# Mamba scan: partitions hold 4 states of 32 channels, sums over states in four column tiles, delta and delta u copied four times through DRAM

## The reference

```
xz = norm(x) @ in_proj_w.T ; x, z = xz[:512], xz[512:]         # 512 channels
u  = silu(conv4(x) + conv_b)
dt_lo, B, C = u @ x_proj_w.T                                    # 64, 16 and 16 wide
delta = softplus(dt_lo @ dt_proj_w.T + dt_proj_b)               # a value per channel and step
step t, for each of 512 channels d and 16 states n:
    h[d,n] = exp(delta[t,d] * A[d,n]) * h[d,n] + delta[t,d] * u[t,d] * B[t,n]
    y[t,d] = sum over n of h[d,n] * C[t,n]
out = ((y + u * D) * silu(z)) @ out_proj_w.T ; x1 = x + out
```

## Time and profile before

| | us |
|---|---|
| median of 3 runs | 3668.91 (3668.2 to 3672.8) |
| the profiled execution, its own time | 3673.93 |
| its span, first to last instruction | 3672.1 |
| busy in the span: PE, DVE, ACT, POOL | 3076.9, 2359.1, 1541.0, 2411.9 |

### The profile page before, as it was taken

The page is one execution under the profiler, slowest core; times in us unless marked ns, Lnnn a source line. Parts: engine busy times, 40 slices in busy tenths (PEclk is TensorE's granted clock), DMA queues, the critical chain, the costliest instruction groups (busy, mean ns, idle before and its releaser), DMA issues. The chain is left out here.

```text
span 3672.1 us, 40492 instructions
## 1 busy us (share of the span) xinstructions
PE 3076.9 (84%) x13154; PEld 1668.5 (45%) x13154; DVE 2359.1 (64%) x2473; ACT 1541.0 (42%) x2519; POOL 2411.9 (66%) x1493
## 2 busy tenths in 40 slices
PE   5988899889988998899887359996888888529998
PEld 2344344334434443444343236663656666416665
DVE  1898888888888888888889552211555555462221
ACT  3555554555555456545654112222334343202221
POOL 1898888888988888878989146662333343217663
PEclk8999999999989999999999669998999999859999
DMA  3022312220232032203221104442011111203343
GB/s 124 32 87 110 116 36 86 110 109 25 103 110 87 34 115 110 87 35 115 104 87 40 52 27 82 83 80 53 25 46 40 46 40 36 75 22 73 81 81 34
DMA packets 120038, 260.62 MB, mean 71 GB/s; under 512 B 15345, under 2 KB 91121, under 8 KB 103378
## 3 DMA queue, kind: packets, MB, share of 16 engines
q1 hardware_dynamic: 91218, 225.29, 16.9%
q0 software_dynamic: 28672, 33.64, 6.0%
HBM read 206.46 MB, written 52.43 MB: 71 GB/s over the span
## 5 line engine op out<-in xcount | busy, mean ns | idle before, releaser
L472 POOL TENSOR_TENSOR m_dbu<-m_du,m_bc 128x1024 f32<-128x1024 f32 x512 | 1192.7, 2357 | 10.3 <-DVE m_dah L552 10.1
L662 PE MATMUL m_y<-m_hc,m_ident 128*128 128x512 f32 x2048 | 992.6, 617 | 20.2 <-POOL m_hc L479 11.3
L552 DVE TENSOR_TENSOR_SCAN m_dah<-m_dah,m_dbu 128x1024 f32<-128x1024 f32 x352 | 804.9, 2287 | 153.9 <-ACT m_dah L297 145.4
L297 ACT ACTIVATE m_dah<-m_delta,m_a_neg 128x512 f32<-128x512 f32 x1024 | 661.9, 681 | 405.6 <-DVE m_hc L563 374.1
L662 PEld LDWEIGHTS m_y<-m_hc,m_ident 128*128 128x128 f32 x2048 | 404.7, 200 | 533.3 <-issue 495.8
L479 POOL TENSOR_TENSOR m_hc<-m_hc,m_bc 128x1024 f32<-128x1024 f32 x160 | 376.5, 2353 | 231.2 <-DVE m_hc L552 231.1
L563 DVE TENSOR_TENSOR m_hc<-m_dah,m_bc 128x1024 f32<-128x1024 f32 x352 | 429.1, 1219 | 14.6 <-PE m_y L662 3.5
L552 DVE TENSOR_TENSOR_SCAN m_hc<-m_dah,m_dbu 128x1024 f32<-128x1024 f32 x160 | 365.1, 2282 | 38.4 <-ACT m_dah L297 38.2
L662 PE MATMUL m_wk<-m_xnT,m_w_in 128*128 128x512 f32 x512 | 244.7, 601 | 11.5 <-DVE m_cw_diag L615 8.8
L662 PE MATMUL m_wk<-m_xs,m_cw_diag 128*128 128x512 f32 x512 | 244.9, 602 | 3.4 <-ACT m_xs L332 3.4
L1136 PE MATMUL f_h<-f_xgT,f_w 128*128 128x512 f32 x512 | 222.3, 595 | 0.0
(11 more groups left out here) (288 smaller groups left out, 4454.7 us busy)
## 6 DMA issues: line engine op xcount, KB each, us to landing
m_bc<-bcd SPq DMA_DIRECT2D x64, 2048.0 KB, 8.2
f_w<-in_w SPq DMA_DIRECT2D x24, 512.0 KB, 4.6
g_w<-in_w SPq DMA_DIRECT2D x24, 512.0 KB, 4.6
m_xt<-in_x SPq DMA_DIRECT2D x16, 512.0 KB, 8.2
m_xr<-in_x SPq DMA_DIRECT2D x16, 512.0 KB, 10.0
x<-m_xr SPq DMA_DIRECT2D x16, 512.0 KB, 3.0
xn<-m_yg SPq DMA_DIRECT2D x16, 512.0 KB, 9.3
t_xt<-x SPq DMA_DIRECT2D x16, 512.0 KB, 3.9
```

The costliest lines, as they stand in the source:

```text
L297: last = nc.scalar.activation(dah[:, un % 2, i * T:(i + 1) * T], delta[:, par, dt, :], ACT.Exp, scale=a_neg[:, dt, n:n + 1])
L472: nc.gpsimd.tensor_tensor(dbu[:, un % RING, :, :], du[:, 2 * hf:2 * hf + 2, :], bc[:, 0, n:n + 1, :].to_broadcast([P, 2, T]), ALU.mult).th ...
L552: nc.vector.tensor_tensor_scan(to, dah[:, un % 2, :], dbu[:, un % RING, :, :].rearrange("p i t -> p (i t)"), 0.0, ALU.mult, ALU.add).then_ ...
L662: return nc.tensor.matmul(out, lhsT, rhs, start=first, stop=last)
```

## The change

The partitions now hold 4 states of 32 channels each (partition = 32 * n + d). A *chunk* c is 128 channels, 8 units. A unit is four states (`st` of `NSET` = 4 sets) of two of the chunk's four blocks q of 32 channels. The work of a unit on ACT, POOL and DVE keeps its shape of 128 x 1024.

- The exponentials and first products need delta and du with each block of 32 channels repeated for the 4 states. `store_dd` stores a half of delta and du (two DMAs of 512 KB) to the DRAM tensor ddd, `load_rep` reads a chunk back four times into `delta_r` and `du_r` (8 DMAs, 2 MB in all), two chunks deep. delta itself has one buffer instead of two.
- B and C need one row for each set of 4 states on a partition: 0.5 MB a set instead of 2 MB a group, in four DMAs.
- The sum over the 4 states of a partition block is a product with `fold` (128 x 32, ones where partition % 32 is the column). Its 32 result rows are one of four column places of y. `total` is now one step for two units, with one product for each of the four blocks q. `d_term`, in slots 2, 10, 18 and 26, and `gate_scores` are written in the same 32-column pieces. y alternates by chunk, and the gate works on one chunk at a time (after scans 15, 19, 29 and 3 of the next batch).
- `ON_POOL` has 8 units instead of 10. Most unit numbers of the helpers are others; xn1t and sc have buffers of their own, so the gate no longer waits for stores.

```diff
+NM = UN // 2
+SB = 32
+NQ = P // SB
+NL = P // SB
+NSET = NS // NL
+NREP = NL
+ON_POOL = (1, 4, 7, 8, 17, 19, 23, 27)
...
-        delta = s.sb("delta", [P, 2, KD, T])
+        delta = s.sb("delta", [P, KD, T])
         du = s.sb("du", [P, KD, T])
 
-        bc = s.sb("bc", [P, 2, NS, T])
+
+        delta_r = s.sb("delta_r", [P, 2, NQ, T])
+        du_r = s.sb("du_r", [P, 2, NQ, T])
+        bc = s.sb("bc", [P, 2, NSET, T])
...
+        xn1t = s.sb("xn1t", [P, TJ, C])
...
-            def load_bc(b, g):
-                if g == 0:
+            def load_bc(b, st):
+                if st == 0:
                     wait_alone(sp_, S["st_bc"], b * 16 + 16, S["tick"])
                 if not below(b, 1):
-                    last = NS + 4 * g + 3
-                    wait_alone(sp_, S["dBu"], (b - 1) * UN + last + 1, S["tick"])
-                    wait_alone(sp_, S["hP"], (b - 1) * NP_ + P_BEFORE[last + 1], S["tick"])
-                    wait_alone(sp_, S["hD"], (b - 1) * ND_ + D_BEFORE[last + 1], S["tick"])
-                rows = slice(4 * g, 4 * g + 4)
-                src = bcd.rearrange("(k n) t -> k n t", k=2)[:, rows, :]
-                sp_.dma_start(bc[:, :, rows, :], src.partition_broadcast(P)).then_inc(S[f"ld_bc{g}"], 16)
+                    last = UN - 2 * (NSET - st) + 2
+                    wait_alone(sp_, S["dBu"], (b - 1) * UN + last, S["tick"])
+                    wait_alone(sp_, S["hP"], (b - 1) * NP_ + P_BEFORE[last], S["tick"])
+                    wait_alone(sp_, S["hD"], (b - 1) * ND_ + D_BEFORE[last], S["tick"])
+                src = bcd.rearrange("(k s n) t -> s n k t", k=2, n=NL)
+                for n in range(NL):
+                    sp_.dma_start(bc[n * SB:(n + 1) * SB, :, st, :], src[st, n].partition_broadcast(SB))\
+                        .then_inc(S[f"ld_bc{st}"], 16)
+
+            def store_dd(b, hf):
+                two = slice(2 * hf, 2 * hf + 2)
+                wait_alone(sp_, S["dz"], b * 2 + hf + 1, S["tick"])
+                if not below(b, 1):
+                    for c in (2 * hf, 2 * hf + 1):
+                        wait_alone(sp_, S[f"ld_r{c}"], b * 2 * 16 * NREP, S["tick"])
+                for k, tile in enumerate((delta, du)):
+                    sp_.dma_start(ddd[k, hf].rearrange("k p t -> p k t"), tile[:, two, :]).then_inc(S[f"st_dd{hf}"], 16)
+
+            def load_rep(b, c):
+
+
+                wait_alone(sp_, S[f"st_dd{c // 2}"], b * 32 + 32, S["tick"])
+                if c >= 2 or not below(b, 1):
+                    used = b * UN + 8 * (c - 1)
+                    wait_alone(sp_, S["dA"], used, S["tick"])
+                    wait_alone(sp_, S["dBu"], used, S["tick"])
+                for k, tile in enumerate((delta_r, du_r)):
+                    src = ddd[k, c // 2, c % 2].rearrange("(q d) t -> d q t", q=NQ)
+                    for n in range(NL):
+                        sp_.dma_start(tile[n * SB:(n + 1) * SB, c % 2, :, :], src).then_inc(S[f"ld_r{c}"], 16)
...
+                if post:
+                    load_rep(b, 1)
                 if ahead(b):
                     wait_alone(sp_, S["tr"], b * 2 + 4, S["tick"])
                     load_x(b + 2)
+                store_dd(b, 1)
+                load_rep(b, 2)
                 if post:
                     store_x1(b - 1)
-                if prep:
-                    store_bc(b + 1)
-                    load_bc(b + 1, 0)
+                load_rep(b, 3)
                 if post:
                     store_xn1(b - 1)
                     load_xr(b)
                 if prep:
+                    store_bc(b + 1)
+                    load_bc(b + 1, 0)
+                    store_dd(b + 1, 0)
+                    load_rep(b + 1, 0)
                     load_bc(b + 1, 1)
-                    load_bc(b + 1, 2)
                 if post:
                     store_sc(b - 1)
                 if prep:
+                    load_bc(b + 1, 2)
                     load_bc(b + 1, 3)
...
-            def scan_exp(b, par, un):
-                hf, n = un // NS, un % NS
-                if n == 0:
-                    act.wait_ge(S["dz"], b * 2 + hf + 1)
+            def scan_exp(b, un):
+                c, st, h = un // 8, un % 8 // 2, un % 2
+                if un % 8 == 0:
+                    act.wait_ge(S[f"ld_r{c}"], (b + 1) * 2 * 16 * NREP)
                 if un >= 2 or not below(b, 1):
                     v, vb = (un - 2) % UN, b - (un < 2)
                     if v in ON_POOL:
@@ -293,11 +329,10 @@
                     else:
                         act.wait_ge(S["hD"], vb * ND_ + D_BEFORE[v] + 1)
...
-                    if post and un in (16, 17):
-                        out_norm3(b - 1, (16, 17).index(un))
+                    if post and un in (20, 27):
+                        out_norm3(b - 1, (20, 27).index(un))
...
-            def times_b(b, par, un):
-                hf, n = un // NS, un % NS
-                if n == 0:
-                    pool.wait_ge(S["du"], b * 2 + hf + 1)
-                if hf == 0 and n % 4 == 0:
-                    pool.wait_ge(S[f"ld_bc{n // 4}"], b * 16 + 16)
+            def times_b(b, un):
+                c, st, h = un // 8, un % 8 // 2, un % 2
+                if un % 8 == 0:
+                    pool.wait_ge(S[f"ld_r{c}"], (b + 1) * 2 * 16 * NREP)
+                if c == 0 and h == 0:
+                    pool.wait_ge(S[f"ld_bc{st}"], (b + 1) * 16 * NL)
                 if not below(b * UN + un, RING):
                     pool.wait_ge(S["scan"], b * UN + un - RING + 1)
-                nc.gpsimd.tensor_tensor(dbu[:, un % RING, :, :], du[:, 2 * hf:2 * hf + 2, :],
-                                        bc[:, 0, n:n + 1, :].to_broadcast([P, 2, T]),
+                nc.gpsimd.tensor_tensor(dbu[:, un % RING, :, :], du_r[:, c % 2, 2 * h:2 * h + 2, :],
+                                        bc[:, 0, st:st + 1, :].to_broadcast([P, 2, T]),
...
                     if post:
-                        if un == 2:
+                        if un == 0:
                             mk_du(b, par, 1)
...
-                    if prep and un == 30:
+                    if prep and un == 28:
                         mk_du(b + 1, 1 - par, 0)
...
-            def gate(b, par, hf):
-                dve.wait_ge(S["sum"], b * UN + (hf + 1) * NS)
-                if hf == 0:
+            def gate(b, par, c):
+                dve.wait_ge(S["sum"], b * NM + c * NSET + NSET)
+                if c == 0:
                     dve.wait_ge(S["sz"], b + 1)
                 if not below(b, 1):
-                    if hf == 0:
+                    if c == 0:
                         dve.wait_ge(S["op"], b * 2)
-                    else:
-                        dve.wait_ge(S["pt"], b * 2)
-                        dve.wait_ge(S["st_xn1"], b * 16)
-                two = slice(2 * hf, 2 * hf + 2)
-                nc.vector.tensor_tensor(yg[:, two, :], y[:], sz[:, par, two, :], ALU.mult).then_inc(S["yg"], 1)
+                nc.vector.tensor_tensor(yg[:, c, :], y[:, c % 2, :], sz[:, par, c, :], ALU.mult).then_inc(S["yg"], 1)
...
+                    if un in (15, 19, 29):
+                        gate(b, par, (15, 19, 29).index(un))
                     if post:
-                        if un == 1:
-                            gate(b - 1, 1 - par, 1)
-                        if un in (9, 10):
-                            residual(b - 1, (9, 10).index(un))
-                        if un in (10, 11):
-                            out_norm1(b - 1, (10, 11).index(un))
-                        if un == 14:
+                        if un == 3:
+                            gate(b - 1, 1 - par, 3)
...
-            def d_term(b, par, hf):
-                if hf == 0:
-                    pe.wait_ge(S["u"], b + 1)
-                if not below(b * 2 + hf, 1):
-                    pe.wait_ge(S["yg"], b * 2 + hf)
-                for i in range(2):
-                    last = mm(y[:, i, :], d_diag[:, 2 * hf + i, :], u[:, par, 2 * hf + i, :], True, False)
-                last.then_inc(S["dm"], 1)
-
-            def total(b, un):
-                wait_h(pe, b, un)
-                for i in range(2):
-                    last = mm(y[:, i, :], ident[:], hc[:, un % RING, i, :], False, un % NS == NS - 1)
+            def d_term(b, par, c):
+                if c == 0:
+                    wait_alone(pe, S["u"], b + 1, S["tick"])
+                if not below(b * 4 + c, 2):
+                    wait_alone(pe, S["yg"], b * 4 + c - 1, S["tick"])
+                for q in range(NQ):
+                    nc.tensor.matmul(y[q * SB:(q + 1) * SB, c % 2, :], d_diag[:, c, q * SB:(q + 1) * SB], u[:, par, c, :],
+                                     start=True, stop=False, skip_group_check=True)
+
+            def total(b, m):
+                c, st = m // NSET, m % NSET
+                for un in (2 * m, 2 * m + 1):
+                    if un in ON_POOL:
```

(23 more changed lines are left out.)

189 lines of the change are left out of this document (97 added, 92 removed).

## The result

The changed kernel takes 3692.1 us (median of four runs, 3687.5 to 3693.2), the kernel before 3668.6 on the same chip: ratio 1.006 [1.0043, 1.0077]. It is 23.5 us slower, where 50 us faster was forecast.

The account below looks back on a forecast made before the run. PE was taken to lead in a ring of waits, with DVE beneath. -189 (DVE) + 43 (waits inside batches) + 90 (edge) + 5 (start) = -51; 3673.9 - 51 = 3623, less 5: 3618, called 3620; range 3545 to 3720.

Parts of the forecast that it names:

- What bounds before: Mamba layer: PE leads in a ring of waits, DVE lies under it; 14.5 us of DVE waits a batch.
- a sign of being right: Mamba stage, after the change: ACT no longer waits for PE by tens of us.
- Sums on PE: PE's `total`: narrow column-placed matmuls take 14.5 us a batch instead of 62; PE's busy time falls from 109 to about 62.
- E: Rival for PE's sums: column tiles don't overlap, sums keep 62 us a batch, 3717 us in all; chance 5%.
- DVE's bound: Mamba layer: DVE needs 109.8 us a batch without waits, 11.8 under the 121.6 of before.
- -189 + 43: Over 16 batches: 189 us gained down to DVE's work, 43 lost to new waits inside batches (2.7 a batch).
- 109.8: DVE's forecast time in us for a batch after the change, without waits.
- The ACT work heaped on units 26 to 29 costs 0.4.: Inside a batch, units 26 to 29: ACT's work there costs 0.4 us of the 2.7 us of waits.
- Copy load: +8.2.: Batch edge: chunk-0 copy load takes 8.2 us, plus 0.4 for eight issues; edge wait 6.0, 90 us over 15 edges.
- The walk: Batch edge from scan 27: stores, B/C loads and copy load in SP's order put the next scan 0 at 23.6 us.
- Rival C: Batch edge: 32-partition copy loads move at half rate, 6.6 us of moving become 13.2, 3743 us in all; chance 16%.
- Rival D: PE idles and its clock drops; ACT's copies in units 11 and 12 come late, costing 48 us, 3668; chance 12%.

Follow-up runs that it names:

- stale-copy kernel: Changed kernel storing delta and du halves only in batch 0, chunk-0 copy load issued early, later copies stale: 3687.7 us against 3833.3 for the kernel before, ratio 0.9611.
- control: The changed kernel as it is, run again on another chip: 3858.5 us against 3835.9 for the kernel before, ratio 1.0066.
- the experiment: Changed kernel with five of ACT's copies one unit later: 3652.7 us against 3669.2 for the kernel before, ratio 0.9956.

## Why the prediction was wrong

*What bounds before: right, as far as shown.* PE's waits for the gate are gone, and so are DVE's 242 us of waits; asking later for PE's results in the kernel before gained nothing. But PE's busy time fell by a quarter, to 67% of the window or 82 us a batch, where 62 and a share near 55% were forecast, and ACT still waits for PE: the two largest rows are 45.6 and 40.7 us from 1000 to 1584, where they were 53.3 and 37.6. The prediction had named the end of such waits as a sign of being right.

*Sums on PE: right in kind, wrong in size.* Eight of the narrow instructions take 1.06 us at full clock, 0.13 each, for the 0.113 of the sum; at the clock that was granted they are 0.164. That the column tiles would not overlap (E) is refuted.

*DVE's bound: right.* -189 + 43 was to be the time with all but the edge; the work grew by 35, the waits of before went. In the stale-copy kernel 1784.5/16 = 111.5 us a batch, less 57.1/16 of waits, leave 108.0 for the 109.8. Of the 43, scan 1 is 1.2 where 1.5 was said, and scans 10 and 11 wait 1.1 together for 0.8, once ACT is out of the way.

*The failing step, first half: "The ACT work heaped on units 26 to 29 costs 0.4."* It took that for all that ACT would cost, since PE was free. The measured 4.6 a batch, 73 us, are 66 more than forecast; scan 28 alone is 0.8 a batch. A free PE is not a prompt PE: it takes its own instructions in order, and a sum that waits for GpSimd holds back the projection behind it. At scans 7 and 13, 19.5 us in all, a slow clock has no visible part: in the three units before them it is 0.9 or more in all but one of the batches of the changed kernel and its control. The change had also moved ACT's copies closer to PE's matmuls, as the unit numbers in both programs say:

| for the next batch | PE before | ACT before | PE after | ACT after |
|---|---|---|---|---|
| in-projection x | 0, 4, 10, 14 | 1, 5, 11, 15 | 0, 2, 10, 12 | 0, 5, 10, 12 |
| convolution, second half | 2, 6, 12, 16 | 4, 8, 14, 18 | 4, 6, 14, 17 | 4, 6, 16, 17 |

Before, every copy stood one or two units behind its matmul; after, six of these eight stand in the same unit, and five of those are the ones moved by the experiment. Only PE's load was reckoned, not when each of its results is asked for. The edit of five unit numbers returned 40 us and took the waits from 64.5 to 9.5 in the window.

*The failing step, second half: "Copy load: +8.2."* The walk was right to within 0.6 us up to there. The copy took 12.3 us to POOL's product and not 8.6, so the wait was 8.8 and not 6.0 at 14 edges (3.7 more for the copy, about 1.0 less because DVE itself came later) and 2.3 at the first: 125 us, not 90. Rival C, the half rate of 32 partitions, was right in kind and too strong: 2.1 of its forecast 6.6 us. The Trainium skill, DMA: Bandwidth & Descriptors, section "The descriptor swizzle", has the lower and upper 64 partitions behind different ports, for one transfer to all 128; the loads sent alternately to both halves, 11.3 us instead of 12.3, agree with it, though that 128-wide loads are faster still leaves room for a finer effect.

*Rival D, the clock: right in kind, and part of the failing step.* The clock fell from 0.93 to 0.81, and the forecast's own sum has nothing for it. At scan 18, with 18.4 us the dearest place, the waits come of the clock: same order, same start, and 0 us at a clock of 1.00. At scan 11, with 12.4 us, the evidence points the same way: the sum, D term and projection before it take 5.5 us in most batches of the changed kernel and 4.4 in the three of the control where the clock was 1.00, and there DVE did not wait; but it did not wait either in two batches at 0.69 in which PE began earlier. The two places make 31 us, where D had said 48, at units 11 and 12. The later copies remove them without a faster clock, so at scan 18 it took both, the early place and the slow clock, to make DVE wait.

The sum as it came out: -242 of waits, +35 of work, +125 edge, +73 ACT, +18 of POOL inside a batch, +3 of DVE for itself, +7 at the start make +19, for a measured 3691.4 - 3672.1 = 19.3 in span. Left open: what a full clock would give in all, and the last 0.5 us between the 9.1 of two wide loads and the 8.6 assumed.

## What to carry to other kernels

When a change frees the engine that led, list for each in-order engine in which step it asks for a result and in which step that result's maker, in its own order, can give it: a schedule that leaned on the old bound hides such places, and shifting five copies by one step gave 40 us, more than the 23 that the change had cost. Where such a chain passes through PE, read the granted clock at that place and not only its mean: the same matmuls took 5.0 or 7.8 us there. A load on the critical path is not priced by its bytes alone: here 2 MB took 9.1 to 12.3 us by the width, the number and the order of its DMAs. And the chain that starts it should be begun as soon as its data exist, which here was worth 83 us for one number.

## What was not expected of the hardware

- 2 MB in eight loads of 32 partitions reach POOL in 12.3 us, in eight of 128 partitions in 10.2, in two in 9.1; the order of the blocks alone is worth 1.0 us.
- While these loads run the DMA engines show as full, 1.06 in the window of the edge, at 224 GB/s.
- Reading the same DRAM rows four times costs no more than reading four sets (12.3 both).
- PE's clock can be raised by useless products, 0.81 to 0.91, and the kernel still loses 42 us.
- The clock granted at one and the same place of the program differs from batch to batch, 0.60 to 1.00, and with it the wait of another engine, 2.2 to 0 us.
